# A partition holds four neighbouring rows of a batch; two copies out of PSUM put the time axis in order

## The reference

```
xn = layernorm(x)                                   # over the 256 columns, no affine part
# state-space branch, per batch
dBC   = xn @ W_deltaBC.T ; delta(64), B(16), C(16) = split(dBC)
delta = softplus(delta @ W_dt.T + b_dt)             # 256 channels
h[t]  = exp(delta[t] * A) * h[t-1] + delta[t] * B[t] * xn[t]     # 16 states per channel, along 512 rows
y[t]  = sum over states of h[t] * C[t]  +  D * xn[t]
# expert branch, per batch
probs = softmax(xn @ Wg.T)                          # 8 experts
G, I  = top 128 of the 512 rows for each expert
out   = G * (gelu(xn[I] @ W1[e] + b1[e]) @ W2[e] + b2[e]), added at rows I
result = x + y + out
```

## Time and profile before

| | us |
|---|---|
| median of 3 runs | 2493.12 (2491.65 to 2495.48) |
| the profiled execution's own time | 2495.35 |
| its span in the trace | 2493.5 |
| DVE busy | 2417.3 (97%) |
| PE busy | 2356.9 (95%) |
| POOL busy | 2200.3 (88%) |
| ACT busy | 1971.3 (79%) |

### The profile page before, as it was taken

The page is one execution under the profiler, slowest core; times in us unless marked ns, Lnnn a source line. Parts: engine busy times, 40 slices in busy tenths (PEclk is TensorE's granted clock), DMA queues, the critical chain, the costliest instruction groups (busy, mean ns, idle before and its releaser), DMA issues. The chain is left out here.

```text
span 2493.5 us, 32910 instructions
## 1 busy us (share of the span) xinstructions
PE 2356.9 (95%) x10524; PEld 1773.7 (71%) x10524; DVE 2417.3 (97%) x2090; ACT 1971.3 (79%) x3432; POOL 2200.3 (88%) x1260
## 2 busy tenths in 40 slices
PE   7828999999999999999999999999999999999996
PEld 3306777777777777777777777777777777777775
DVE  6599999999999999999999999999999999999995
ACT  6627888888888888888888888888888888888783
POOL 4316999999999999999999999999999999999996
PEclk9958999999999999999999999999999999999998
DMA  9872455444445453454535344444444445453443
GB/s 303 274 270 69 136 167 140 117 124 112 135 117 137 102 137 108 117 132 98 154 99 146 95 133 107 127 123 117 133 116 125 108 115 133 100 150 93 106 91 53
DMA packets 162973, 325.38 MB, mean 130 GB/s; under 512 B 16272, under 2 KB 133104, under 8 KB 146160
## 3 DMA queue, kind: packets, MB, share of 16 engines
q1 hardware_dynamic: 95536, 239.11, 28.0%
q0 software_dynamic: 66048, 83.92, 20.1%
q10 hardware_dynamic: 1216, 0.23, 0.0%
HBM read 250.84 MB, written 84.93 MB: 135 GB/s over the span
## 5 line engine op out<-in xcount | busy, mean ns | idle before, releaser
L494 POOL TENSOR_TENSOR ysum<-ysum,prod 128x1024 f32<-128x1024 f32 x480 | 1307.1, 2723 | 33.4 <-DVE prod L905 24.4
L896 DVE TENSOR_TENSOR_SCAN bank_x<-decay,bank_x 128x1024 f32<-128x1024 f32 x512 | 1167.2, 2280 | 0.0
L1102 PE MATMUL bank_l<-ext,w_sb 128*128 128x256 f32 x4096 | 970.3, 382 | 0.8 <-ACT og L688 0.8
L1121 PE MATMUL bank_l<-w_sb,hid 128*128 128x256 f32 x4096 | 957.2, 383 | 0.0
L1121 PEld LDWEIGHTS bank_l<-w_sb,hid 128*128 128x128 f32 x4096 | 762.6, 190 | 163.4 <-issue 67.7
L1102 PEld LDWEIGHTS bank_l<-ext,w_sb 128*128 128x128 f32 x4096 | 756.5, 190 | 136.2 <-issue 23.5
L638 ACT ACTIVATE hid<-bank_l,b_all 128x256 f32<-128x256 f32 x1024 | 430.9, 475 | 332.6 <-PE bank_l L1102 329.4
L629 ACT ACTIVATE decay<-delta,a_sb 128x511 f32<-128x511 f32 x1024 | 640.0, 708 | 1.2
L905 DVE TENSOR_TENSOR prod<-bank_x,c_all 128x1024 f32<-128x1024 f32 x512 | 620.4, 1212 | 0.1
L842 DVE TENSOR_TENSOR bank_x<-du,bank_b 128x1024 f32<-128x1024 f32 x512 | 613.4, 1198 | 0.0
L513 POOL DMA_INDIRECT out<-og,idx_all x256 | 408.6, 1596 | 49.5 <-POOL ysum L494 35.4
(11 more groups left out here) (95 smaller groups left out, 1577.9 us busy)
## 6 DMA issues: line engine op xcount, KB each, us to landing
c_all<-c_rows SPq DMA_DIRECT2D x128, 1024.0 KB, 5.4
w_sb<-in_w SPq DMA_DIRECT2D x32, 1024.0 KB, 6.2
decay<-in_x SPq DMA_DIRECT2D x32, 512.0 KB, 5.4
xn_rows<-decay SPq DMA_DIRECT2D x32, 512.0 KB, 4.0
out<-yrow POOLq DMA_DIRECT2D x32, 512.0 KB
xr<-xn_rows SPq DMA_DIRECT2D x30, 512.0 KB, 6.5
ex<-xn_rows,idx_all POOLq DMA_INDIRECT x256
out<-og,idx_all POOLq DMA_INDIRECT x256, 4.1
```

The costliest lines, as they stand in the source:

```text
L494: nc.gpsimd.tensor_tensor(ysum[:, m % 2], first, prod[:, i], ALU.add).then_inc(sum_done, 1)
L896: nc.vector.tensor_tensor_scan(bank_x[:, s % 2], decay[:, k % 2, i].rearrange("p c t -> p (c t)"), bank_x[:, s % 2], 0.0, ALU.mult, ALU.ad ...
L1102: i = nc.tensor.matmul(bank_l[(q + k) % 2][:, (f % 2) * UT:(f % 2 + 1) * UT], w1_sb[:, e2, hc, f * P:(f + 1) * P], ext[:, k % 2, hc], star ...
L1121: i = nc.tensor.matmul(o, hid[:, (k - 1) % 2, f, c * K:(c + 1) * K], w2_sb[:, le2, f], start=False, stop=(f == FC - 1 and c == UB - 1))
```

## The change

Three DRAM access patterns are turned: partition p now holds rows 4p to 4p + 3 of a batch, so that its four chunks are 4 KB side by side in DRAM too. Chunk c, partition p is row 4p + c. What PE then transposes is out of time order, each block of 128 columns holding every fourth row; the two ACT copies out of PSUM read it in order and write it with a step of four elements (16 bytes), which puts time in order in `xtr` and `xnt`. On the way back, PE's stationary operand of `y_rows` is read from `ysum` with a step of four elements. The DMAs of lines 293, 297, 315 and 526 keep their bytes, their number and their waits.

```diff
-        x_tiles = x.rearrange("b (c p) d -> b p c d", p=P)
+        x_tiles = x.rearrange("b (p c) d -> b p c d", p=P)
-        out_tiles = out.rearrange("b (c p) d -> b p c d", p=P)
-        xn_tiles = xn_rows.rearrange("(b c p) d -> b p c d", p=P, c=TC)
+        out_tiles = out.rearrange("b (p c) d -> b p c d", p=P)
+        xn_tiles = xn_rows.rearrange("(b p c) d -> b p c d", p=P, c=TC)
...
-                        nc.scalar.copy(xtr[:, par], tr_banks[par]).then_inc(xnt_done, 2)
+                        nc.scalar.copy(xtr[:, par].rearrange("p h (r c) -> p h c r", c=TC),
+                                       tr_banks[par].rearrange("p h (c r) -> p h c r", c=TC)).then_inc(xnt_done, 2)
...
-                nc.scalar.copy(xnt[:, par, dt], bank_t[:]).then_inc(xnt_in[par], 16 // HC)
+                nc.scalar.copy(xnt[:, par, dt].rearrange("p (r c) -> p c r", c=TC),
+                               bank_t[:].rearrange("p (c r) -> p c r", c=TC)).then_inc(xnt_in[par], 16 // HC)
...
-                                                ysum[:, par, dt, c * P:(c + 1) * P], ident[:])
+                                                ysum[:, par, dt, :].rearrange("p (r c) -> p c r", c=TC)[:, c], ident[:])
```

## The result

The changed kernel takes 2500.91 us (median of 8 runs, 2498.84 to 2505.29), the kernel before 2494.18 us in the same comparison. The ratio is 1.0028, 95% interval 1.0017 to 1.0038: 6.7 us more, where 6 us less was forecast. That is rival B's side. The profiled execution took 2505.29 us, the slowest of the eight: its trace is 10.0 us longer than the one before, 3.3 us more than the typical loss.

The account below looks back on a forecast made before the run. Transfers were taken to bound the rows stage and DVE the scan. Stage -4, its end +0.7, kernel's end -3 sum to -6 us: 2487.1 us against the median, own range 2483 to 2491, 8 in 10 range 2479 to 2500.

Parts of the forecast that it names:

- rival B: ACT's strided write costs more than one extra element time; at three times, rows stage 4.02 per batch, 2506.7 us; chance 0.17.
- I take 3.25 per batch.: Rows stage: pace in us per batch, down from 3.42 over 25 batches, a gain of 4 us.
- three limits: Rows stage, us per batch: ACT 3.12, PE 3.07, DMA 2.99, so close that their waits add up.
- the copy's price: Line 567, rows stage: the 16-byte step adds 0.70 us, ends 0 and 0.80, a copy of 1.69 us.
- the 0.40 named: Line 648, scan: the most each 512-element copy would grow, in us; 0.35 expected, absorbed by ACT's idle time.
- the prediction's own rule: Rows stage: ACT needs 2.42 us per batch plus the step's price; the pace was taken at 3.25 against ACT's 3.12.
- The stage's end: After 96 us: nothing gained, and the last batch's longer copy is on the path to the logits; loss 0.7 us.
- the limit of 2.99: Rows-stage transfers, us per batch: 4 KB packets at 173 ns make 2.77, with the extras 2.99.
- PE's 3.07: Rows stage: PE's need in us per batch, 1.07 + 1.90 and a tenth for the softmax's small transposes.
- Rival C: Transfers gain nothing, by the 512 B rule or loop latency; stage stays at 3.42, 2491.8 us; chance 0.16.
- The scan: Lines 648 and 1001: longer copies and weight loads (up to 280 ns) are covered, so the scan's length stays unchanged.
- The kernel's end: Behind the last scan: the two last yrow DMAs gain 1.5 us each, 3 us in all.

Follow-up runs that it names:

- step_alone: Kernel before with only the two ACT copies writing with a 16-byte step, pieces of 1 KB; 2503.36 us, ratio 1.0039.
- eight_steps: Kernel before with line 567's copy taking turns in eight forms of write or read step; ran once, read for durations and pace alone.
- plain_copies: Changed kernel with both ACT copies out of PSUM left plain, time out of order; 2492.39 us, ratio 0.9998.
- step_on_read: Changed kernel with both ACT copies writing SBUF in order and reading PSUM with a step, same result; 2493.71 us, ratio 0.9997.
- time_off_chain: Kernel before with one more plain ACT copy of 1024 elements per rows-stage batch, that nothing waits for; 2496.82 us, ratio 1.0013.
- read_late_logits: step_on_read with DVE's copy of every fourth batch's logits moved behind the statistics and shift; 2489.76 us, ratio 0.9983.

## Why the prediction was wrong

*"I take 3.25 per batch."* This is the step that failed: the stage's pace, the largest of three limits plus 0.13, forecast as a gain of 4 us. It was 3.70 us per batch, a loss of 7.1 us in the profiled execution, and 3.63 in step_alone. Three things were wrong in it: the copy's price, the gain credited to the transfers, and a term that was missing, the copy's place on the chain.

*The copy's price.* The term was 0.70 us with 0.80 as its end; it measured 1.00 (eight_steps, plain 994 ns to 1999 ns). The bound from the nearest row came from another engine and from a copy of 128 elements, whose time without a step had to be guessed from a slope; it gave the direction and too small a size. Doubling ACT's own slope was closer. What a 16-byte step adds is about 1.0 ns per element in both copies: 1.00 us on 1024, 0.51 on line 648's 512, above the 0.40 named. This alone turns the sign of the stage's term: by the prediction's own rule the pace becomes 2.42 + 1.00 + 0.13 = 3.55, 3.3 us slower instead of 4 faster, and by its other terms the whole sum would have come out near +1.

*The copy's place.* The sum priced ACT's copy by ACT's busy time. With the copy at 1.99 us ACT's limit is about 3.3 (its copies start 3.26 us apart when nothing is awaited, 3.45 with the small activation), and the pace was 3.70; with plain copies PE's is 3.07, and the pace was 3.33 in plain_copies and 3.41 in step_on_read, not 3.12. time_off_chain and step_alone have nearly the same ACT load and lose 3.3 and 9.8 us: the copy counts mostly by where it lies, on the way from the transposes over the copy and the gate matmuls to DVE's logits. How much of that is waiting and how much the lower clock behind the loads (*The stage's end* below) stays open. Rival B had the direction and put its turning point at a copy of 2.0 us by ACT's sum alone; at 1.99 the rows stage had already lost 7.1 us in the trace.

*The 4 KB pieces.* The stage was read as bound by its transfers, from a DMA share of 1.00 and a sum of packets that gave the pace; the limit of 2.99 rested on that. The packets are 8% shorter (185 ns against 202) and the DMA engines have idle time, yet plain_copies and step_on_read, which have them without the longer copy, tie with before: no gain in the stage is clear of the noise. Part of the term was mis-sized: at 185 ns a batch's transfers are 256 x 185 / 16 + 0.22 = 3.18 us, not 2.99, so in plain_copies they are still the largest of the three limits, above PE's 3.07. Rival C said that they gain nothing. Its first reason, the 512 B rule of the Trainium skill (DMA: Bandwidth & Descriptors, Specifications), is not why: the packets do differ. Its second, a loop that passes on only the landing time, is not shown: the landing time fell by only 0.1 to 0.2 us, which would fit, but read_late_logits lands later at the same pace. What takes up the rest of the gain stays open.

*The stage's end* was put at +0.7. In the profiled execution it is +4.6, in part this execution's own; in step_alone it is +2.3 and in time_off_chain -2.1. The window of 100 to 125 us in the kernel after (columns as above):

```profile
100.00:125.00 25.00, 20.39 (x70) 8.34 (x69) 9.03 (x47) 17.98 (x24) 7.80 (x10) 0.79 0.61 219
```

TensorE's granted clock is 0.79 of full, so for some 40% of the stretch it is at 1.2 GHz instead of 2.4; the kernel before has 0.93 there, step_alone, in an execution near its median, 0.86, time_off_chain 1.00. Two batches' gate matmuls take 3.2 and 3.6 us in it instead of 1.9; the kernel before has one such batch, at 2.9. The prediction had no term for the clock. Whether PE's waits for ACT bring these falls about was not tested.

*What held.* The scan: 2259.95 to 2260.62 us between the same two points in all eleven timed kernels' traces, with the longer copies and weight loads (203 ns, below the 280 allowed) inside their covers. The kernel's end: 3 us were taken, 1.5 measured (0.6 and 0.9); POOL's instruction is 0.43 us shorter both times (2.00 to 1.57, 1.37 to 0.94; 1.0 and 0.4 were taken), and the last DMA ends 7.2 us after its issue instead of 8.1, so its transfer gained 0.5 us of the 4.3 estimated: accumulation does go nearly by bytes here.

Sum by medians: y side -1.7, loads and stores in 4 KB pieces about 0 (plain_copies has both and is at -1.1), stepped copies +8 (the change against plain_copies) to +10 (step_alone), against the +6.7 measured.

Still open: why the pace is 0.3 us above PE's 3.07, and 0.15 to 0.2 above the transfers' 3.18, when ACT is light and the transfers have idle time (93.1% busy in plain_copies). No single wait was found that holds it there.

## What to carry to other kernels

When a permutation has to happen in a copy out of PSUM, walk it so that SBUF is written without a gap and PSUM is read with the step, or let PE write the step: the same result was free both ways and cost 1 us per 1024 float32 elements the other way, once the step was 16 bytes. Before pricing a faster transfer by its bytes, do not take a DMA share of 1.00 as proof that the stage follows the bytes: here packets 8% shorter brought no gain clear of the noise. And where several engines are as close to the pace as here, price a longer instruction by the chain it lies on, not by its engine's busy sum.

## What the runs showed of the hardware that was not expected

ACT writing float32 to SBUF with a step: 994 ns for 1024 elements plain, 1058 with 8 bytes, 1552 (1020 elements) with 12, 1999 with 16, 1888 with 64, 1935 with 512. Reading PSUM with a step of 16 or 512 bytes: 992. PE's transposes writing PSUM with a step of 16 bytes: a median of 273 ns, as without. PE's weight load of 128 columns read with a step of 16 bytes: 203 ns against 140. POOL's instruction for an accumulating DMA of 512 KB: a median of 1.95 us with 512 pieces of 1 KB, 1.52 with 128 of 4 KB.
